# Layer 0 of a four-layer convolution and attention kernel: v computed with its weights stationary, and the attention output product on it

## The reference, cut to what matters

```
y  = group_norm(x)
b  = conv1x1(y, w_qkv)                              # 576 channels
d  = concat(dwconv3(b), dwconv5(b), dwconv7(b))     # 1728 channels
q, k, v = split(conv1x1(d, w_pconv), 3)             # 192 channels each
attn = l2norm(q) @ l2norm(k).T * temperature        # 8 heads, 24 x 24 over channels
a = sum over three top-k masked softmaxes of attn, scaled
x = x + conv1x1(a @ v, w_proj)
```

## Time and profile before

| what | value |
|---|---|
| median of 3 runs | 2782.25 us (2777.99 to 2783.22) |
| the profiled execution, its own time | 2779.78 us |
| its span in the trace | 2777.9 us |
| TensorE busy | 2059.9 us, 74% of the span |
| VectorE, ScalarE, GpSimd busy | 1303.1, 1022.2, 849.1 us |
| pointwise stage of layer 0 (line 675) | 647.0 to 1322.3 us |
| product of attention and v (lines 764 to 816) | 1361.7 to 1449.4 us |

### The profile page before, as it was taken

The page is one execution under the profiler, slowest core; times in us unless marked ns, Lnnn a source line. Parts: engine busy times, 40 slices in busy tenths (PEclk is TensorE's granted clock), DMA queues, the critical chain, the costliest instruction groups (busy, mean ns, idle before and its releaser), DMA issues. The chain is left out here.

```text
span 2777.9 us, 38167 instructions
## 1 busy us (share of the span) xinstructions
PE 2059.9 (74%) x16032; PEld 1257.4 (45%) x16032; DVE 1303.1 (47%) x1197; ACT 1022.2 (37%) x1444; POOL 849.1 (31%) x446
## 2 busy tenths in 40 slices
PE   3768787767999999999489658777678678772032
PEld 1466665665777777777235222222223223221021
DVE  5334344341011010111450265798889799979703
ACT  2344444440000000000132236667676766655110
POOL 1333323220000000000000120687688678873300
PEclk9989898878999999999699779899899899996555
DMA  5899999987331331310300041000000000013399
GB/s 167 256 270 279 247 309 233 271 228 210 93 107 57 104 107 54 107 54 1 96 3 7 7 134 23 0 0 0 0 1 0 0 0 0 0 50 93 142 226 279
DMA packets 157448, 292.93 MB, mean 105 GB/s; under 512 B 10284, under 2 KB 135212, under 8 KB 151084
## 3 DMA queue, kind: packets, MB, share of 16 engines
q1 hardware_dynamic: 144620, 284.39, 36.1%
q10 hardware_dynamic: 12672, 6.29, 0.8%
HBM read 168.16 MB, written 120.91 MB: 104 GB/s over the span
## 5 line engine op out<-in xcount | busy, mean ns | idle before, releaser
L675 PE MATMUL ps<-mem 128*128 128x288 f16 x5376 | 653.9, 287 | 19.5 <-DMA mem<-depthwise_out 19.5
L675 PEld LDWEIGHTS ps<-mem 128*128 128x128 f16 x5376 | 501.8, 98 | 157.5 <-DMA mem<-depthwise_out 19.7
L1650 POOL TENSOR_TENSOR mem<-mem 128x1024 f32<-128x1024 f32 x192 | 460.6, 2412 | 86.1 <-ACT mem L1579 85.7
L1551 PE MATMUL ps<-mem 128*128 128x512 f32 x768 | 388.2, 630 | 12.9 <-POOL mem L1650 12.1
L500 PE MATMUL ps<-mem 56*96 56x240 f16 (+1 forms) x5184 | 311.8, 282 | 107.6 <-DVE mem L606 98.3
L1679 DVE TENSOR_TENSOR_SCAN mem<-mem,ps 128x1024 f32<-128x1024 f32 x144 | 335.8, 2332 | 89.7 <-issue 50.7
L500 PEld LDWEIGHTS ps<-mem 56*96 56x96 f16 x5184 | 300.5, 130 | 133.9 <-DVE mem L606 106.0
L1072 POOL TENSOR_TENSOR mem<-mem 128x1536 f16<-128x1536 f32 x16 | 50.8, 3179 | 996.3 <-ACT mem L1052 996.3
L715 DVE TENSOR_TENSOR mem<-mem 128x384 f32<-128x384 f32 x64 | 35.7, 559 | 610.8 <-ACT mem L729 610.8
L606 DVE TENSOR_TENSOR mem<-ps,mem 96x1024 f16<-96x1024 f32 x144 | 171.2, 1216 | 225.2 <-ACT mem L545 224.0
L727 ACT COPY mem<-ps 128x288 f32<-128x288 f32 x64 | 25.5, 398 | 645.7 <-PE ps L675 645.7
(11 more groups left out here) (204 smaller groups left out, 2119.0 us busy)
## 6 DMA issues: line engine op xcount, KB each, us to landing
depthwise_out<-mem SPq DMA_DIRECT2D x108, 512.0 KB, 8.1
mem<-depthwise_out SPq DMA_DIRECT2D x32, 1664.0 KB, 9.9
mem<-base_phases SPq DMA_DIRECT2D x72, 448.0 KB
base_phases<-mem SPq DMA_DIRECT2D x56, 512.0 KB, 9.6
mem<-in_wd SPq DMA_DIRECT2D x72, 336.0 KB
mem<-l_planes SPq DMA_DIRECT2D x48, 252.0 KB
mem<-in_x SPq DMA_DIRECT2D x4, 2048.0 KB, 11.0
l_planes<-mem SPq DMA_DIRECT2D x2, 4032.0 KB, 13.3
```

The lines of the kernel that those rows point to most:

```text
L675: ins = nc.tensor.matmul(ps[:, 2 * (i % 2) + h, 0:HALF], d, pw[rows, wa, k, HALF * h:HALF * h + HALF], start=(k == 0 and n == 0), stop=(k ...
L1551: ins = nc.tensor.matmul(py[:, a, :], ident, hh[:, n % 4, 512 * a:512 * a + 512], start=(n % N == 0), stop=(n % N == N - 1))
L1650: nc.gpsimd.tensor_tensor(hh[:, n % 4, :], hh[:, n % 4, :], cs[:, n % 2, :], ALU.mult).then_inc(hc_pool, 1)
```

## The change

v is taken out of the pixel-stationary product and gets one of its own, in which the weights are stationary and 256 moving columns are the pixels of two phases of one image, so that v comes out with its channels on partitions. Its 192 channels stand in two tiles of 128 channels (one per image, PSUM banks 4 and 5) and in one bank in which the last 64 channels of the two images share the partitions (bank 7). q and k keep the old form, with 384 columns in one bank instead of 288 in two, and four banks in turn instead of two pairs. Blocks are taken in pairs: the last row of channels of both blocks stands side by side behind the rest. v is split into high and low parts as it leaves PSUM, in `vall`, and the product with attention is a `product_block` that reads these parts, with no transposes, no split of its input and no f32 matmuls other than those for the small matrix.

```
     # layer0_pointwise, SyncE: when a slot is free
-                    sp.wait_ge(acc_done, 4 * (j - NSLOT + 1))
+                    sp.wait_ge(v_sum, j - NSLOT + 1)
     # TensorE
+            def vconv(j):
+                if j:
+                    pe.wait_ge(v_lo, j)
+                last = NK - 1
+                for k in range(NK):
+                    d = dbuf[:, j % NSLOT, k].rearrange("p (f a b n) -> p a b f n", f=2, a=2, b=B)
+                    for n, (a, wa) in enumerate(PASSES):
+                        first, final = k == 0 and n == 0, k == last and n == 2
+                        for b in range(B):
+                            rows = slice(64 * b, 64 * b + 64) if k == last else slice(0, 128)
+                            nc.tensor.matmul(v_tiles[:, b], pw[rows, wa, k, 2 * C:2 * C + 128], d[rows, a, b],
+                                             start=first, stop=final, skip_group_check=True)
+                        for b in range(B):
+                            rows = slice(64 * b, 64 * b + 64) if k == last else slice(0, 128)
+                            ins = nc.tensor.matmul(v_rest[64 * b:64 * b + 64], pw[rows, wa, k, 2 * C + 128:3 * C], d[rows, a, b],
+                                                   start=first, stop=final, skip_group_check=True)
+                ins.then_inc(v_sum, 1)
+
             def pconv(i):
...
+                if i >= 4:
+                    pe.wait_ge(qkv_out, i - 3)
+                for k in range(NK - 1):
+                    for n, (a, wa) in enumerate(PASSES):
+                        nc.tensor.matmul(qk_psum(i), pixels(i, a, k, slice(0, 128)), pw[:, wa, k, 0:2 * C], ...)
+            def pconv_last(i):
+                k = NK - 1
+                for n, (a, wa) in enumerate(PASSES):
+                    for m in range(2):
+                        rows = slice(64 * m, 64 * m + 64)
+                        ins = nc.tensor.matmul(qk_psum(i + m), pixels(i + m, a, k, rows), pw[rows, wa, k, 0:2 * C], ...)
...
-            for i in range(NBLK):
-                if i % 2 == 0:
-                    j = i // 4
-                    pe.wait_ge(d_loaded[j % NSLOT][i // 2 % 2], 48 * (j // NSLOT + 1))
+            for i in range(0, NBLK, 2):
+                j = i // 4
+                pe.wait_ge(d_loaded[j % NSLOT][i // 2 % 2], 48 * (j // NSLOT + 1))
                 pconv(i)
+                pconv(i + 1)
+                pconv_last(i)
                 if i:
+                    gram(i - 2)
                     gram(i - 1)
+                if i % 4 == 2:
+                    vconv(j)
+            gram(NBLK - 2)
             gram(NBLK - 1)
     # VectorE, after the squares of block i
+                if i % 4 == 3:
+                    j = i // 4
+                    s = slice(256 * j, 256 * j + 256)
+                    dve.wait_ge(v_hi, j + 1)
+                    nc.vector.tensor_tensor(vall[:, 1, 0:2, s], ps[:, 4:6, 0:256], vall[:, 0, 0:2, s], ALU.subtract)
+                    nc.vector.tensor_tensor(vall[:, 1, 2, s], ps[:, 7, 0:256], vall[:, 0, 2, s], ALU.subtract).then_inc(v_lo, 1)
     # ScalarE: one copy a block instead of three, and v's high part once a step
-                nc.scalar.copy(qkv[:, i % 2, 0:HALF], ps[:, bank, 0:HALF])
-                nc.scalar.copy(qkv[:, i % 2, HALF:2 * C], ps[:, bank + 1, 0:2 * C - HALF])
-                nc.scalar.copy(vall[:, PHASES * (i % 2) + i // 2, :], ps[:, bank + 1, 2 * C - HALF:HALF]).then_inc(qkv_out, 1)
+                nc.scalar.copy(qkv[:, i % 2], ps[:, i % 4, 0:2 * C]).then_inc(qkv_out, 1)
+                if i % 4 == 3:
+                    v_high(i // 4)
     # layer0_attention: the small matrix goes straight into product_block's form
-            for bh in range(BH):
-                ins = nc.tensor.matmul(ps[0:HC, bh, 0:C], attn_w[0:HC, bh, :], wp[0:HC, bh % 2, :], start=True, stop=True)
+            for b in range(B):
+                second = attn_w[0:HC, 2 * b + 1]
+                nc.tensor.matmul(ps[0:HC, b, 0:C], attn_w[0:HC, 2 * b, :], wp[0:HC, 0, :], start=True, stop=True)
+                nc.tensor.matmul(ps[HC:128, b, 0:C], second[:, 0:128 - HC], wp[0:HC, 1, :], start=True, stop=True)
+                ins = nc.tensor.matmul(ps[64 * b:64 * b + 64, 2, 0:C], second[:, 128 - HC:HC], wp[0:HC, 1, :], start=True, stop=True)
...
+            nc.scalar.copy(mm.rearrange("p (b c) -> p b c", b=3), ps[:, 0:3, 0:C])
+    product_block(nc, sem, ar, ps, "l0", None, mm, (0, C), 2 * C, xt, stats, x_wait=(x_loaded, 64),
+                  parts=(vall[:, 0], vall[:, 1]), scale=1.0, block_of=block_of)
     # product_block, VectorE: with block_of the sum goes to x through a reordered view
+                        if block_of is None:
+                            V.scalar_tensor_tensor(out=o, in0=p, scalar=1.0 / SCALE, in1=o, op0=ALU.mult, op1=ALU.add).then_inc(added, 1)
+                        else:
+                            V.tensor_tensor(o, p.rearrange("p (f y x) -> p y x f", y=16, x=8), o, ALU.add).then_inc(added, 1)
```

More of the change, by code:

```diff
@@ L638, in layer0_pointwise @@
     ones = ar.take(1)
-    assert ar.at <= ar.size - NBLK * C
+    assert ar.at <= ar.size - NT * HW
     NJ = PHASES // 2
-    HALF = QKV // 2
     d_loaded = [[sem("l0_depthwise_loaded") for _ in range(2)] for _ in range(NSLOT)]
     acc_done = sem("l0_pconv_done")
+    v_sum = sem("l0_v_in_psum")
+    v_hi = sem("l0_v_high_part")
+    v_lo = sem("l0_v_low_part")
     qkv_out = sem("l0_qkv_in_sbuf")
@@ L665, in _ @@
         def _(pe):
-            def pconv(i):
[L667 to L677, removed]
+            PASSES = ((0, 0), (0, 1), (1, 0))
@@ new lines, in qk_psum, with pixels @@
+            def qk_psum(i):
+                return ps[:, i % 4, 0:2 * C]
+            def pixels(i, a, k, rows):
+                j, f, b = i // 4, i // 2 % 2, i % 2
+                c0 = 512 * f + 256 * a + 128 * b
+                return dbuf[rows, j % NSLOT, k, c0:c0 + 128]
+            def vconv(j):
[15 more added lines that the diff above has]
+                ins.then_inc(v_sum, 1)
@@ new lines, in pconv @@
+            def pconv(i):
+                if i >= 4:
+                    pe.wait_ge(qkv_out, i - 3)
+                for k in range(NK - 1):
+                    for n, (a, wa) in enumerate(PASSES):
+                        nc.tensor.matmul(qk_psum(i), pixels(i, a, k, slice(0, 128)), pw[:, wa, k, 0:2 * C], start=(k == 0 and n == 0), stop=False)
+            def pconv_last(i):
[3 more added lines that the diff above has]
+                        rows = slice(64 * m, 64 * m + 64)
+                        ins = nc.tensor.matmul(qk_psum(i + m), pixels(i + m, a, k, rows), pw[rows, wa, k, 0:2 * C], start=False, stop=(n == 2))
+                        if n == 2:
+                            ins.then_inc(acc_done, 1)
@@ L740, in layer0_attention @@
     attention(nc, sem, ar, ps, inp, ident, gacc, attn_w, 0, (xt, xin, x_loaded))
-    m0 = ar.take(BH, C)
     wp = ar.take(2, C)
-    vs = ar.take(4, 512)
-    assert ar.at <= ar.size - NBLK * C
+    mm = ar.take(3 * C)
     wp_loaded = sem("l0_wproj_loaded")
     m_sum = sem("l0_m_in_psum")
[L748 to L753, removed]
     with nc.Block() as block:
@@ L791, in _ @@
             act.wait_ge(m_sum, 1)
[L792 to L835, removed]
@@ L987, in product_block, with operand, block @@
         loaded = [sem(f"{tag}_residual_loaded") for _ in range(2)]
-    else:
+    elif x_to is not None:
         stored = sem(f"{tag}_stored")
+    def operand(xa, t, k):
+        return x16[k % 2][:, xa, t] if parts is None else parts[xa][:, t, 512 * k:512 * k + 512]
+    def block(t, k):
+        return xt[:, t, 512 * k:512 * k + 512] if block_of is None else block_of(t, k)
     out_free, out0 = (added, q0) if x_from is None else (bias_in, 0)
-    with nc.Block() as block:
-        @block.sync
+    with nc.Block() as program:
+        @program.sync
         def _(sp):
@@ L1009, in _ @@
                             sp.dma_start(x_to[b, c0:c0 + n, s], xt[p0:p0 + n, t, s]).then_inc(stored, 16)
-        @block.tensor
+        @program.tensor
         def _(pe):
@@ L1016, in _ @@
             for k in range(NK):
-                x = x16[k % 2]
                 def bank(t):
@@ L1029, in _ @@
                     for n, (a, xa) in enumerate(PASSES):
-                        nc.tensor.matmul(out[t], w16[a][:, ia[t]:ia[t] + 128], x[:, xa, t], start=(n == 0), stop=False)
+                        nc.tensor.matmul(out[t], w16[a][:, ia[t]:ia[t] + 128], operand(xa, t, k), start=(n == 0), stop=False)
                 for n, (a, xa) in enumerate(PASSES):
@@ L1033, in _ @@
                         p = slice(64 * t, 64 * t + 64)
-                        ins = nc.tensor.matmul(out[t], w16[a][p, ic:ic + 128], x[p, xa, 2], start=False, stop=(n == 2))
+                        ins = nc.tensor.matmul(out[t], w16[a][p, ic:ic + 128], operand(xa, 2, k)[p], start=False, stop=(n == 2))
                         if n == 2:
@@ L1039, in _ @@
```

(18 more changed lines are left out.)

81 lines of the change are left out of this document (38 added, 43 removed).

## The result

| | kernel before | changed kernel |
|---|---|---|
| median of the runs | 2782.73 us (4 runs, 2777.99 to 2785.88) | 2891.23 us (4 runs, 2882.7 to 2893.89) |
| ratio | | 1.0386, 95% interval 1.0359 to 1.0414 |
| the profiled execution | 2779.78 us | 2882.70 us |
| its span | 2777.9 us | 2880.8 us |
| forecast | | 2882 us, range 2855 to 2912 |

The kernel is slower by 3.9%, inside the range. Between the two profiled executions the difference is 102.9 us, where 101 had been summed. It can be laid out by stage, from the points at which each stage begins.

A forecast was written before the change was run, and what follows sets the result against it. TensorE alone was taken to bound the pointwise stage, and VectorE to set the new product's pace. From 2779.8 us, plus 143 for the pointwise stage, minus 42 for the product, 2881; from the median 2883. Forecast 2882 us, range 2855 to 2912.

The forecast's parts named there:

- Columns: Pointwise stage: the columns stay the same as before within 1%, as the array was full and stays full.
- The price of a change: In v's product each change of array form costs 0.113 us, bounds 0.10 and 0.13; 84 changes a step, 9.5 us.
- What hides: Pointwise stage: new ScalarE and VectorE work, vconv's wait for v_lo and SyncE's wait for v_sum stay hidden.
- The product: Product with attention, 88.0 us before: the stage ends 42 us earlier.
- The small matrix: Start of the product stage, at the lower clock: 12 records and five changes of 0.35 us, about 6 us in all.
- Block 0: First block of the product with attention: 7.4 us at the lower clock, twice 3.7.
- the pace: Product blocks after block 0: VectorE sets it at 3.8 us a block, against TensorE's 3.7.
- slow read of PSUM: Product's sum reading PSUM at a 512-byte step: 0.69 us taken; at the bound of 1.0 the stage is 7 us longer.
- lone changes of form might be hidden: Rival for v's product: vconv runs at its columns, a step takes 41.8 us, 2733 us in all; chance 6%.
- the 64-column pair stands side by side: Assumed in v's product; the rival that it doesn't adds 68 us, 2950 us in all, chance 4%.
- The clock stayed at 1.00 in vconv: Rival: the clock falls in v's product, 3186 us if wholly at 1.2 GHz, 2983 for a third; chance 6%.
- The product stage did not keep its length: Rival for the product with attention: it keeps its length through slow strided reads or late x, 2925 us; chance 3%.

The follow-up runs named there:

- g_all: Changed kernel with v's matmuls reordered, all in the 128-column form, then all in the 64-column form: median 2740.13 us, ratio 0.9851 to the kernel before.
- split_pair: Changed kernel with one 64-column matmul put behind each 128-column one, so 4 changes of form a pass in place of 2: 3111.75 us (one run).
- one_pass: Changed kernel with one pass in place of three in layer 0's product with attention, low parts left out: 2878.41 us (one run).

## Why the prediction was right

**The path.** That TensorE alone bounds the pointwise stage held: the difference of the stage, 143.4 us, is 16 times the difference of a step (9.06) less the shorter tail.

**Columns.** The sum said that the columns stay the same within 1%. g_all shows it: with 80 of v's 84 changes of form gone, the step is 42.11 us against 42.12.

**The price of a change.** 0.113 us was taken as the mean over three groups in layer 1's product, and the trace of before had it only behind three slots or more. It measured 0.113 and 0.114 in the two differences of order, and 0.44 us for a pair of single slots in split_pair. The mean held. The single change is not 0.113, though: by the starts above it costs 0.10 us out of a form with 128 columns and 0.12 us out of one with 64, and v's product has as many of one as of the other. The prediction averaged three groups in which both kinds occur, without asking which is which, so that the agreement to 1 ns is in part luck. The bounds of 0.10 and 0.13 enclosed the single changes, and for a mean were wider than needed.

**What hides.** ScalarE's and VectorE's new work, the wait for v_lo and SyncE's wait for v_sum cost nothing that can be seen: TensorE is busy for 200 of 200 us, and, as busy time could hide a gap, the better sign is that a step takes 51.18 us where its terms without any wait sum to 51.15.

**The product.** The sum had 42 us, rounded down from 42.7, and it was 46.1. Two terms were too large, both at the lower clock. The small matrix took 5.1 us from its first matmul to the copy (1508.33 to 1513.43), where 6 were reckoned: the last of its six groups starts 4.16 us after the first, ten records of 0.32 us and five changes of 0.19, not 0.35. Block 0 took 5.65 us (1515.96 to 1521.62) and not 7.4, because the clock rose within it: the granted clock was 0.50 from 1516 to 1519 us, 0.77 on the mean from there to 1521.6, and 1.00 after that. And the pace was TensorE's at 3.69 us, not VectorE's at 3.8, which makes 0.8 us in seven blocks. Here the prediction had the wrong engine. Its three sums in 1.99 us came out as forecast, but they hold a wait: the third starts 0.71 us after the second, against 0.60 in one_pass, where the three take 1.87 us. The bound for a slow read of PSUM did not come into play (0.681 us on the median), as the read in order takes 0.692 us on the mean. The page that spoke for it (the Trainium skill, SBUF — State Buffer, Specifications (TRN2)) gives no price for such a crossing, and for this read by VectorE the trace shows none.

**The rivals.** That lone changes of form might be hidden is ruled out by the passes of 0.55 us and by split_pair, which also shows that the 64-column pair stands side by side. The clock stayed at 1.00 in vconv. The product stage did not keep its length.

## What to carry to other kernels

Count changes of the array's form (128 rows or 64, 128 columns or 64) as a cost of their own. Here, in half precision and with a granted clock of 1.00, they took 0.113 us each on the mean, with 256 or 512 moving columns, and beside a slot of 256 columns (0.109 us) that is a second slot. The cure is order, not another algorithm: matmuls of one form after each other, with one PSUM bank for each form so that sums can stay open, took 9.07 us a step, 145 in all, out of this change without touching a single matmul, and turned a loss of 3.9% into a gain of 1.5%. The busy time of TensorE shows nothing of it; the starts of the weight loads do, which then stand at their own matmul instead of under the one before.

## What the runs showed of the hardware that was not expected

- A change of form costs 0.113 us on the mean from 84 to 28 changes, and 0.114 from 28 to 4. The single change costs 0.10 us out of a form with 128 columns of the array and 0.12 us out of one with 64, for 256 moving columns (0.32 and 0.23 us from start to start in the changed kernel) as for 512 (line 1034 to 1040 in 0.75 us, 1040 to 1044 in 0.77).
- VectorE read PSUM with a step of 512 bytes between elements in 0.681 us for 512, as fast as in order (0.692 on the mean).
- An untouched stage ahead of the change ended up to 8.6 us apart in the traces of four kernels; a difference of 3 us in a later stage can be read from its steps and not from the medians.
